# Graph attention on one core: first x tiles projected in two parts, row 0 spread by TensorE, adjacency turned later

## The chip, the cores and the metric

One core of one Trainium2 chip. The metric is the device time of one execution in microseconds (us), lower is better. The core's engines are TensorE (PE in the profile, its weight loads PEld), VectorE (DVE), ScalarE (ACT), GpSimd (POOL) and SyncE (SP), which issues DMAs.

## What is computed

```python
N, D_IN, H, DH, ALPHA, MASK_VAL = 2048, 512, 16, 32, 0.2, -65500.0
seq = (x @ W_seq).reshape(N, H, DH)
score1 = einsum('nhd,d->hn', seq, a1)
score2 = einsum('nhd,d->hn', seq, a2)
scores = leaky_relu(score1[:, :, None] + score2[:, None, :], negative_slope=ALPHA)
scores = scores + (1.0 - adj)[None, :, :] * MASK_VAL
attn = softmax(scores, axis=-1)
hidden = einsum('hij,jhd->ihd', attn, seq).reshape(N, D_IN)
out = layernorm(x + elu(hidden @ W_out + b_out), axis=-1)
```

x is 2048 x 512, adj is 2048 x 2048 of zeros and ones, all float32.

## The kernel before

All engines run programs written out by hand; they meet only through semaphores, and each engine executes its own program strictly in order. Nodes are cut into NT = 16 tiles of 128.

**First stage (to about 91 us), by tile t.** SP loads x tiles into a ring of six buffers and adjacency tiles (1 MB each) into a ring of four, after W (four chunks of 256 KB) and the two small broadcast loads of a1 and a2 (lines 219 and 220, between the first and the second chunk of W). VectorE and POOL multiply W by a1 and a2 (L514, L758) and VectorE sums the products over each head (L519) into 16 extra columns of each half of Wx, so that one product of x with Wx gives seq and both scores. For each tile:

- turn_x(t) on TensorE (L270) transposes x tile t, four 128x128 transposes into bank t % 2; ScalarE's copy_x (L406) brings it to xT.
- project(t) (L282) multiplies it by Wx: 8 matmuls of 272 columns in float32, recorded as 16 passes, each with a weight load. It waits for x_copied, for seq_copied of tile t - 2 (its PSUM banks), and at t = 0 for wa_ready of each k, that is for VectorE's sums.
- cast_adj(t) on ScalarE (L413) turns adjacency tile t to 8 bits and sums its rows; fix_adj(t) on VectorE (L525, L528) handles rows without edges.
- turn_adj(t) on TensorE (L292) transposes the tile, eight transposes, into bank 6 + t % 2; copy_adj(t) brings it to adj8, on VectorE for even tiles (L559), on ScalarE for odd ones (L419). turn_adj(t) waits for adj_fixed and, from t = 2 on, for the copy of tile t - 2 (adj_ready).
- copy_ab(t) and copy_seq(t) on VectorE (L534 to L543) empty the projection's banks; largest (L551, L553) follows each fourth tile.

TensorE's order is turn_x(t + 1), project(t), turn_adj(t). ScalarE's is copy_x(t + 1), cast_adj(t), and at even t copy_adj(t - 1). VectorE's is fix_adj(t), at odd t copy_adj(t - 1), copy_ab(t), copy_seq(t).

**Turn to the heads (91 to 103 us).** turn_a (L298) transposes the first score into rows, one per head; ScalarE copies them to aT (L431), SP stores aT to a DRAM scratch in four pieces (L230), waits for x_turned and the stores, and loads the row of head 0 back to all 128 partitions in four pieces of 256 KB (L234). Rows 1 to 15 follow as one load of 1 MB each (L241). aT lies in the first 16 partitions of row 1's buffer. Meanwhile the maxima go through TensorE (mx_turned, mx_spread; L318, L322), VectorE and ScalarE make E (L583, L437, L439) and Es (L595), VectorE writes the scale column of seq (L600), and values(0) (L605) makes the first value tile.

**Heads (to about 500 us).** For each head and tile, VectorE (L653) or ScalarE (L471) compares the head's row with a column of ab, VectorE ANDs the result with adj8 (L667), and TensorE multiplies by V (L332, mask_products), with adj_products (L344) between. split_high and split_low (L444, L611) make V. The last stage normalizes, multiplies by W_out (L394), and applies elu and the layer norm.

## Time and profile before

| | us |
|---|---|
| median of 3 runs | 570.86 |
| lowest, highest | 568.2, 571.78 |
| the profiled execution | 573.0 |
| its span | 571.1 |
| its mean granted clock of TensorE | 0.971 |

The span goes from the first to the last recorded instruction; the execution's own time has 1.9 us around it. Line numbers in the profile are those of the kernel before. An arrow in a row names what is written and what is read (tring<-abc,ab), "<-" behind idle time what ended it. Clock figures are tenths or shares of full speed, 1.0 being 2.4 GHz.

### The profile page before, as it was taken

How to read it: one execution, taken by the hardware profiler on the slowest of the kernel's cores; microseconds unless marked ns; L12 is line 12 of the kernel's file. 1: busy time of each engine (PE TensorE's matmuls, PEld its weight loads, DVE VectorE, ACT ScalarE, POOL GpSimd, SP SyncE). 2: the span in 40 equal slices, each digit the busy share in tenths (PEclk: the TensorE clock that was granted, in tenths of full speed). 3: DMA queues.
4: the chain of work that ended last, by engine and by line, in shares of the span. 5: the costliest groups of instructions: out<-in, count | busy, mean ns of one | idle time of the engine just before them, and what ended most of it. 6: DMA issues, size and time to landing. Idle time of an engine off the chain costs nothing.

```text
span 571.1 us, 15331 instructions
## 1 busy us (share of the span) xinstructions
PE 520.7 (91%) x6803; PEld 468.1 (82%) x6803; DVE 503.9 (88%) x804; ACT 420.7 (74%) x384; POOL 38.6 (7%) x63
## 2 busy tenths in 40 slices
PE   2999993757999999999999999999999999799992
PEld 2688882657999999999999999999999999544440
DVE  3878687999897969699999999989998979879997
ACT  1567684999696978799999998999996966122230
POOL 4000000000000000000000000000000000334432
PEclk9999997796999999999999999999999999899997
DMA  7988614010201202020211201102012030013433
GB/s 259 414 307 287 227 56 152 7 75 1 76 1 76 71 8 76 2 75 2 76 36 43 76 2 76 75 3 76 2 76 76 2 130 2 1 55 110 141 119 129
DMA packets 14194, 49.64 MB, mean 87 GB/s; under 512 B 1776, under 2 KB 2800, under 8 KB 10160
## 3 DMA queue, kind: packets, MB, share of 16 engines
q1 hardware_dynamic: 14128, 48.67, 23.9%
q8 instruction: 53, 0.87, 0.6%
q14 instruction: 13, 0.11, 0.1%
HBM read 44.34 MB, written 4.33 MB: 85 GB/s over the span
## 4 chain that ended last, share of the span: by engine, by line
PE 68%; DVE 19%; ACT 5%; issue 4%; DMA 2%; POOL 1%; SPq 1%; POOLq 0%; DVEq 0%; ACTq 0%
PE sums L332 38%; PE bank L344 19%; PE sums L282 6%; DVE tring L667 2%; ACT tring L471 2%; DVE tring L653 2%; PE sums L394 2%; DVE Vp L731 2%; DVE Vp L718 2%; DVE Vp L741 2%; DVE Vp L737 1%; DVE adj L559 1%; PE bank L292 1%; DMA abc<-a_rows 1%; ACT tring L413 1%
## 5 line engine op out<-in xcount | busy, mean ns | idle before, releaser
L471 ACT ACTIVATE tring<-abc,ab 128x2048 int8<-128x2048 f32 x157 | 304.2, 2003 | 4.6 <-DMA abc<-a_rows 4.6
L332 PE MATMUL sums<-Vp,tring 128*128 128x132 f16 x4096 | 257.5, 228 | 21.2 <-DVE Vp L611 10.0
L332 PEld LDWEIGHTS sums<-Vp,tring 128*128 128x128 fp8e4 x4096 | 252.4, 100 | 23.1 <-issue 18.3
L667 DVE TENSOR_TENSOR tring<-adj,tring 128x512 uint32<-128x512 uint32 x256 | 167.4, 690 | 10.5 <-ACT tring L471 10.3
L653 DVE TENSOR_SCALAR tring<-abc,ab 128x2048 int8<-128x2048 f32 x99 | 127.1, 1284 | 2.1 <-DMA abc<-a_rows 2.1
L344 PE MATMUL bank<-Vp,adj 128*128 128x132 f16 x2048 | 126.0, 221 | 0.9 <-ACT acc L450 0.9
L344 PEld LDWEIGHTS bank<-Vp,adj 128*128 128x128 fp8e4 x2048 | 122.3, 96 | 1.0 <-issue 1.0
L282 PE MATMUL sums<-Vp,abc 128*128 128x272 f32 x256 | 63.6, 401 | 1.2 <-DVE Vp L519 1.2
L394 PE MATMUL sums<-abc,Vp 128*128 128x512 f32 x128 | 59.2, 607 | 0.8
L282 PEld LDWEIGHTS sums<-Vp,abc 128*128 128x128 f32 x256 | 48.4, 195 | 11.4 <-DVE Vp L519 2.3
L506 ACT ACTIVATE Vp<-Vp 128x512 f32<-128x512 f32 x16 | 10.1, 631 | 50.1 <-DVE Vp L727 50.1
L461 ACT ACTIVATE low<-sums 128x66 f32<-128x66 f32 (+3 forms) x33 | 18.0, 596 | 38.5 <-PE sums L332 38.5
L394 PEld LDWEIGHTS sums<-abc,Vp 128*128 128x128 f32 x128 | 23.5, 194 | 26.8 <-issue 23.5
L626 DVE SCALAR_TENSOR_TENSOR cab<-low,sums 128x33 f32<-128x33 f32 (+3 forms) x66 | 23.3, 419 | 18.1 <-ACT low L461 18.1
L413 ACT ACTIVATE tring<-Vp 128x2048 int8<-128x2048 f32 x16 | 30.6, 1913 | 2.1 <-DMA Vp<-in_adj_dram 2.1
L406 ACT COPY abc<-sums 128x512 f32<-128x512 f32 x16 | 9.4, 586 | 30.4 <-PE sums L270 30.4
L763 POOL MEMSET Vp<- 128x128 f32 x1 | 0.2, 204 | 428.0 <-PE sums L332 428.0
L450 ACT ACTIVATE acc<-bank 128x132 f32<-128x132 f32 x64 | 16.9, 282 | 8.8 <-PE bank L344 8.8
L611 DVE SCALAR_TENSOR_TENSOR Vp<-Vp,xp 128x528 f16<-128x528 f16 (+1 forms) x34 | 21.3, 672 | 0.0
L605 DVE TENSOR_TENSOR xp<-acc,Es 128x1056 f32<-128x1056 f32 (+1 forms) x17 | 20.2, 1192 | 0.1
L270 PE MATMUL sums<-Vp,abc 128*128 128x128 f32 x64 | 10.7, 294 | 10.1 <-DMA abc<-in_x_dram 10.1
L444 ACT ACTIVATE Vp<-xp 128x528 f16<-128x528 f32 (+1 forms) x34 | 19.5, 634 | 0.0
(69 smaller groups left out, 304.0 us busy)
## 6 DMA issues: line engine op xcount, KB each, us to landing
Vp<-in_adj_dram SPq DMA_DIRECT2D x16, 1024.0 KB, 6.9
abc<-a_rows SPq DMA_DIRECT2D x15, 1024.0 KB, 4.6
abc<-in_x_dram SPq DMA_DIRECT2D x16, 256.0 KB, 6.3
Vp<-in_x_dram SPq DMA_DIRECT2D x16, 256.0 KB, 2.9
out_dram<-Vp SPq DMA_DIRECT2D x16, 256.0 KB, 2.2
Vp<-in_L_gnn_W_seq_dram SPq DMA_DIRECT2D x4, 256.0 KB, 6.2
abc<-a_rows SPq DMA_DIRECT2D x4, 256.0 KB, 3.7
abc<-in_L_gnn_W_out_dram SPq DMA_DIRECT2D x1, 1024.0 KB, 5.4
```

What stands on the lines that cost most here:

```text
L282: mm = pe.matmul(bank[2 + 2 * s + r][:, 0:WC], xT[:, r, k * P:(k + 1) * P], Wx[:, k, s, :], start=(k == 0), stop=(k == KT - 1))
L332: mm = pe.matmul(bank[b][:, 0:4 * BW].rearrange("p (v c w) -> p v c w", v=4, c=ITB)[:, :, c, :], slot(jt)[:, it * P:(it + 1) * P].bitcast( ...
L344: mm = pe.matmul(bank[6 + s % 2][:, 0:GRP * HW], adj8[:, jt, it * P:(it + 1) * P].bitcast(F8), Vp[:, GRP * g:GRP * (g + 1), jt, part, HW:V ...
L394: mm = pe.matmul(bank[q], hT[:, q, k * P:(k + 1) * P], Wo_sb[:, k, :], start=(k == 0), stop=(k == KT - 1))
L413: act.activation(tring[:, it, :], stage[:, it % STAGE, :], ACT.Copy, bias=BASE, scale=EDGE, accum_out=deg[:, r:r + 1]).then_inc(adj_cast, 1)
L444: high = act.activation(Vp[:, k, tiles, 0, s * HW:(s + 1) * HW], xp[:, tiles, s, :], ACT.Copy, scale=1.0 / LO[s])
L471: act.activation(slot(jt), row(h), ACT.Sign, bias=ab[:, jt, H + h:H + h + 1], scale=-1.0).then_inc(u_ready, 1)
L605: dve.tensor_tensor(xp[:, tiles], seq[:, tiles, k, :].unsqueeze(2).to_broadcast([P, n, 2, HW]), Es[:, tiles, :, k:k + 1].to_broadcast([P, ...
L611: low = dve.scalar_tensor_tensor(out=Vp[:, k, tiles, 1, s * HW:(s + 1) * HW], in0=Vp[:, k, tiles, 0, s * HW:(s + 1) * HW], scalar=-LO[s], ...
L626: both = dve.scalar_tensor_tensor(out=into, in0=lo, scalar=1.0 / LO[s], in1=high, op0=ALU.mult, op1=ALU.add)
L653: dve.tensor_scalar(slot(jt), row(h), ab[:, jt, H + h:H + h + 1], -1.0, ALU.is_gt, ALU.mult).then_inc(above, 1)
L667: dve.tensor_tensor(words, adj8[:, jt, :].bitcast(U32), words, ALU.bitwise_and).then_inc(t_ready, 1)
```

## The change

- **First tiles.** project() takes a range of columns. Tiles 0 and 1 are projected on their first 256 columns as soon as W and x are there, and the last 16 columns (a1, a2) follow for both, after turn_x(2). In the second part the matmuls don't wait for x again, and start=True is given once, in the first part. The loads of a1 and a2 are issued by ScalarE at its start instead of by SP.
- **Adjacency.** TURNS gives the adjacency tiles that TensorE turns at each t: none at 0 and 1, then tile t - 2 up to t = 5, two at t = 6 and at t = 7, and tile t from 8 on. The copies follow one iteration later in ScalarE's and VectorE's orders, behind cast_adj and fix_adj.
- **Row 0.** Each piece of aT's first row is multiplied by a row of ones on TensorE (spread_row0) and copied by ScalarE (copy_row0) into row(0). SP's four loads and its wait for x_turned go. Row 1's load waits for row0_spread. The maxima's transposes move from banks 0 and 1 to bank 6.
- **Scale column.** POOL writes the scale column of seq; VectorE waits for scales_set before values(0).

```diff
@@ -44,6 +44,8 @@
 
 FIVE, SIX, SEVEN = (1, 4, 7, 10, 13), (1, 4, 6, 9, 11, 14), (1, 3, 6, 8, 10, 12, 14)
 DVE_TILES = (SIX, SIX, SEVEN, SEVEN, SIX, SIX, SIX, FIVE, SIX, SIX, SIX, FIVE, SIX, SEVEN, SEVEN, SEVEN)
+
+TURNS = ((), (), (0,), (1,), (2,), (3,), (4, 5), (6, 7)) + tuple((t,) for t in range(8, NT))
 
 MID, MID_AT = 2, 7
 ROUNDS = (0, 5, 5, 6, 4, 4, 4, 4, 4, 4, 4, 4, 5, 5, 6, 0)
@@ -152,12 +154,12 @@
             sem(s) for s in ("x_turned", "x_copied", "seq_made", "ab_copied", "seq_copied"))
         adj_cast, noedge_set, adj_fixed, adj_turned = (sem(s) for s in ("adj_cast", "noedge_set", "adj_fixed", "adj_turned"))
         adj_ready = [sem("adj_ready0"), sem("adj_ready1")]
-        a_turned, a_copied = sem("a_turned"), sem("a_copied")
+        a_turned, a_copied, row0_spread, row0_copied = (sem(s) for s in ("a_turned", "a_copied", "row0_spread", "row0_copied"))
         a_stored = [sem(f"a_stored{c}") for c in range(4)]
         ones_set, mx_part, mx_ready, mx_turned, mcol_ready, diag_ready, mx_spread, Mb_ready = (
             sem(s) for s in ("ones_set", "mx_part", "mx_ready", "mx_turned", "mcol_ready", "diag_ready", "mx_spread", "Mb_ready"))
         e_in, e_out, r_sum, r_in, r_out = (sem(s) for s in ("e_in", "e_out", "r_sum", "r_in", "r_out"))
-        vsc_step, e_scaled = sem("vsc_step"), sem("e_scaled")
+        vsc_step, scales_set, e_scaled = sem("vsc_step"), sem("scales_set"), sem("e_scaled")
 
         xp_made, high_made, v_ready = sem("xp_made"), sem("high_made"), sem("v_ready")
 
@@ -197,7 +199,10 @@
 
         def row_loaded(eng, h):
 
-            eng.wait_ge(abc_loaded[h % 2], 16 * (h // 2 + 1) + (48 if h % 2 == 0 else 0))
+            if h == 0:
+                eng.wait_ge(row0_copied, 4)
+            else:
+                eng.wait_ge(abc_loaded[h % 2], 16 * ((h + 1) // 2))
 
 
         @block.sync
@@ -215,9 +220,6 @@
             load_x(0)
             for k in range(KT):
                 sp.dma_start(Wx[:, k, :, 0:half], W_seq[k * P:(k + 1) * P, :].rearrange("p (s c) -> p s c", s=2)).then_inc(w_loaded[k], 16)
-                if k == 0:
-                    sp.dma_start(a12[:, 0:DH], a1.rearrange("(o d) -> o d", o=1).partition_broadcast(P)).then_inc(a12_loaded, 16)
-                    sp.dma_start(a12[:, DH:2 * DH], a2.rearrange("(o d) -> o d", o=1).partition_broadcast(P)).then_inc(a12_loaded, 16)
             for t in range(1, XS - 2):
                 load_x(t)
             for t in range(NT):
@@ -228,11 +230,9 @@
             for c in range(4):
                 sp.wait_ge(a_copied, c + 1)
                 sp.dma_start(scratch[:, c * 512:(c + 1) * 512], aT[:, c * 512:(c + 1) * 512]).then_inc(a_stored[c], 16)
-            sp.wait_ge(x_turned, NT)
             for c in range(4):
                 sp.wait_ge(a_stored[c], 16)
-                sp.dma_start(row(0)[:, c * 512:(c + 1) * 512],
-                             scratch[0:1, c * 512:(c + 1) * 512].partition_broadcast(P)).then_inc(abc_loaded[0], 16)
+            sp.wait_ge(row0_spread, 4)
             for h in range(1, H):
                 if h == 1:
                     sp.wait_ge(seq_made, NT)
@@ -270,18 +270,23 @@
                     mm = pe.transpose(bank[r][:, k * P:(k + 1) * P], xs[:, t % XS, k * P:(k + 1) * P], idf)
                 mm.then_inc(x_turned, 1)
 
-            def project(t):
+            def project(t, columns=slice(0, WC)):
+
                 r = t % 2
-                pe.wait_ge(x_copied, t + 1)
-                if t >= 2:
-                    pe.wait_ge(seq_copied, t - 1)
+                if columns.start == 0:
+                    pe.wait_ge(x_copied, t + 1)
+                    if t >= 2:
+                        pe.wait_ge(seq_copied, t - 1)
                 for k in range(KT):
-                    if t == 0:
+                    if t == 0 and columns.start == 0:
+                        pe.wait_ge(w_loaded[k], 16)
+                    if t == 0 and columns.start > 0:
                         pe.wait_ge(wa_ready, 2 * k + 2)
                     for s in range(2):
-                        mm = pe.matmul(bank[2 + 2 * s + r][:, 0:WC], xT[:, r, k * P:(k + 1) * P], Wx[:, k, s, :],
-                                       start=(k == 0), stop=(k == KT - 1))
-                mm.then_inc(seq_made, 1)
+                        mm = pe.matmul(bank[2 + 2 * s + r][:, columns], xT[:, r, k * P:(k + 1) * P], Wx[:, k, s, columns],
+                                       start=(k == 0 and columns.start == 0), stop=(k == KT - 1), skip_group_check=(t < 2))
+                if columns.stop == WC:
+                    mm.then_inc(seq_made, 1)
 
             def turn_adj(it):
                 r = it % 2
@@ -300,10 +305,17 @@
                         mm.then_inc(a_turned, 1)
 
             turn_x(0)
-            for t in range(NT - 1):
+            project(0, slice(0, half))
+            turn_x(1)
+            project(1, slice(0, half))
+            turn_x(2)
+            for t in range(2):
+                project(t, slice(half, WC))
+            for t in range(2, NT - 1):
                 turn_x(t + 1)
                 project(t)
-                turn_adj(t)
+                for it in TURNS[t]:
+                    turn_adj(it)
             pe.wait_ge(x_copied, NT)
             pe.wait_ge(ab_copied, NT // 2)
             turn_a(range(0, NT // 2))
@@ -313,14 +325,22 @@
             turn_adj(NT - 1)
             pe.wait_ge(ab_copied, NT)
             turn_a(range(NT - 1, NT))
+            def spread_row0(c):
+
+                pe.wait_ge(a_copied, c + 1)
+                pe.matmul(turned_a[c], ones[0:1, :], aT[0:1, c * 512:(c + 1) * 512], start=True, stop=True).then_inc(row0_spread, 1)
+
+            pe.wait_ge(ones_set, 1)
+            spread_row0(0)
             pe.wait_ge(mx_ready, 1)
-            pe.wait_ge(a_copied, 1)
-            pe.transpose(bank[0][0:2 * H, 0:P], mx, idf).then_inc(mx_turned, 1)
-            pe.wait_ge(ones_set, 1)
+            pe.wait_ge(adj_ready[0], NT // 2)
+            pe.transpose(bank[6][0:2 * H, 0:P], mx, idf).then_inc(mx_turned, 1)
+            spread_row0(1)
             pe.wait_ge(diag_ready, 1)
-            pe.wait_ge(a_copied, 2)
-            pe.matmul(bank[1][:, 0:2 * H], ones[0:2 * H, :], diag[0:2 * H, :], start=True, stop=True).then_inc(mx_spread, 1)
-            pe.wait_ge(a_copied, 4)
+            pe.matmul(bank[6][:, 0:2 * H], ones[0:2 * H, :], diag[0:2 * H, :], start=True, stop=True).then_inc(mx_spread, 1)
+            spread_row0(2)
+            spread_row0(3)
+            pe.wait_ge(row0_copied, 4)
             pe.wait_ge(seq_copied, NT)
             pe.wait_ge(Mb_ready, 1)
             for s in range(2):
@@ -398,6 +418,9 @@
 
         @block.scalar
         def _(act):
+            act.dma_start(a12[:, 0:DH], a1.rearrange("(o d) -> o d", o=1).partition_broadcast(P)).then_inc(a12_loaded, 16)
+            act.dma_start(a12[:, DH:2 * DH], a2.rearrange("(o d) -> o d", o=1).partition_broadcast(P)).then_inc(a12_loaded, 16)
+
             def copy_x(t):
                 r = t % 2
                 act.wait_ge(x_turned, t + 1)
@@ -424,19 +447,29 @@
                 if t + 1 < NT:
                     copy_x(t + 1)
                 cast_adj(t)
-                if t % 2 == 0 and t > 0:
-                    copy_adj(t - 1)
+                if t > 0:
+                    for it in TURNS[t - 1]:
+                        if it % 2 == 1:
+                            copy_adj(it)
             def copy_a(c):
                 act.wait_ge(a_turned, c + 1)
                 act.copy(aT[:, c * 512:(c + 1) * 512], turned_a[c][0:H, :]).then_inc(a_copied, 1)
 
             for c in range(4):
                 copy_a(c)
+            def copy_row0(c):
+                act.wait_ge(row0_spread, c + 1)
+                act.copy(row(0)[:, c * 512:(c + 1) * 512], turned_a[c]).then_inc(row0_copied, 1)
+
             copy_adj(NT - 1)
+            copy_row0(0)
+            copy_row0(1)
             act.wait_ge(e_in, 1)
             act.activation(E[:, :, 1, :], E[:, :, 0, :], ACT.Exp, scale=-SLOPE).then_inc(e_out, 1)
             act.wait_ge(e_out, 1)
             act.activation(E[:, :, 0, :], E[:, :, 0, :], ACT.Exp, scale=-1.0).then_inc(e_out, 1)
+            copy_row0(2)
+            copy_row0(3)
 
             def split_high(k, tiles=slice(0, NT)):
                 act.wait_ge(xp_made, k + 2 if k > 0 else tiles.stop // (NT // 2))
@@ -561,8 +594,10 @@
 
             for t in range(NT):
                 fix_adj(t)
-                if t % 2 == 1:
-                    copy_adj(t - 1)
+                if t > 0:
+                    for it in TURNS[t - 1]:
+                        if it % 2 == 0:
+                            copy_adj(it)
                 copy_ab(t)
                 if t < NT - 1:
                     copy_seq(t)
@@ -573,11 +608,11 @@
             dve.tensor_reduce(mx, mxc.rearrange("p c k -> p k c"), AX.X, ALU.max).then_inc(mx_ready, 1)
             copy_seq(NT - 1)
             dve.wait_ge(mx_turned, 1)
-            dve.tensor_reduce(mcol[0:2 * H, :], bank[0][0:2 * H, 0:P], AX.X, ALU.max).then_inc(mcol_ready, 1)
+            dve.tensor_reduce(mcol[0:2 * H, :], bank[6][0:2 * H, 0:P], AX.X, ALU.max).then_inc(mcol_ready, 1)
             dve.wait_ge(mcol_ready, 1)
             dve.tensor_scalar(diag[0:2 * H, :], idf[0:2 * H, 0:2 * H], mcol[0:2 * H, :], None, ALU.mult).then_inc(diag_ready, 1)
             dve.wait_ge(mx_spread, 1)
-            dve.tensor_copy(Mb, bank[1][:, 0:2 * H]).then_inc(Mb_ready, 1)
+            dve.tensor_copy(Mb, bank[6][:, 0:2 * H]).then_inc(Mb_ready, 1)
             dve.wait_ge(Mb_ready, 1)
             Mrow = Mb[:, 0:H].unsqueeze(1).to_broadcast([P, NT, H])
             dve.tensor_tensor(E[:, :, 0, :], ab[:, :, H:2 * H], Mrow, ALU.add).then_inc(e_in, 1)
@@ -595,10 +630,9 @@
                 dve.scalar_tensor_tensor(out=Es[:, :, s, :], in0=E[:, :, s, :], scalar=LO[s],
                                          in1=vinv.unsqueeze(1).to_broadcast([P, NT, H]), op0=ALU.mult,
                                          op1=ALU.mult).then_inc(e_scaled, 1)
-
+            dve.wait_ge(e_scaled, 2)
+            dve.wait_ge(scales_set, 1)
             dve.wait_ge(seq_copied, NT)
-            dve.tensor_copy(seq[:, :, :, DH], vsc[:].unsqueeze(1).to_broadcast([P, NT, H])).then_inc(e_scaled, 1)
-            dve.wait_ge(e_scaled, 3)
 
             def values(k, tiles=slice(0, NT)):
                 n = tiles.stop - tiles.start
@@ -759,6 +793,10 @@
                                    Wx[:, k, :, 0:half].rearrange("p s (h d) -> p s h d", d=DH),
                                    a12[:, DH:2 * DH].unsqueeze(1).unsqueeze(1).to_broadcast([P, 2, H // 2, DH]), ALU.mult).then_inc(wa_prod[1], 1)
 
+
+            pool.wait_ge(vsc_step, 2)
+            pool.wait_ge(seq_copied, NT)
+            pool.tensor_copy(seq[:, :, :, DH], vsc[:].unsqueeze(1).to_broadcast([P, NT, H])).then_inc(scales_set, 1)
             pool.wait_ge(t_free, NT * (H - 2))
             pool.memset(idl, 0.0).then_inc(ident_l, 1)
             pool.wait_ge(ident_l, 1)
```

## Rows read from the trace of the kernel before

**Rows 1.** The page: busy times, clock in 40 slices, and one group (busy, mean ns)

```profile
PE 520.7 (91%) x6803; PEld 468.1 (82%) x6803; DVE 503.9 (88%) x804; ACT 420.7 (74%) x384; POOL 38.6 (7%) x63
...
PEclk9999997796999999999999999999999999899997
...
L282 PEld LDWEIGHTS sums<-Vp,abc 128*128 128x128 f32 x256 | 48.4, 195 | 11.4 <-DVE Vp L519 2.3
```

**Rows 2.** The chain of waits in order of time: start us, us, what

```profile
2.49 5.89 DMA adj<-in_L_gnn_a_dram
...
16.86 1.29 DVE Vp L519 x2
...
38.83 3.67 PE sums L282 x16
...
57.39 3.67 PE sums L282 x16
...
92.93 6.44 DMA abc<-a_rows
```

**Rows 3.** Timeline, 3 to 25 us: start, us, engine, line, tiles, shape, count, idle before

```profile
3.60 1.09 PE L270 MATMUL sums<-Vp,abc 128*128 128x128 f32 x4 [3.60 <-DMA abc<-in_x_dram]
...
11.18 1.11 PE L270 MATMUL sums<-Vp,abc 128*128 128x128 f32 x4 [6.49 <-DMA abc<-in_x_dram]
...
12.08 3.72 PE L282 MATMUL sums<-Vp,abc 128*128 128x272 f32 x8
...
16.28 1.19 PE L282 MATMUL sums<-Vp,abc 128*128 128x272 f32 x4 [0.48 <-DVE Vp L519]
...
19.61 0.43 PEld L270 LDWEIGHTS sums<-Vp,abc 128*128 128x128 f32 x4
19.66 0.61 PE L270 MATMUL sums<-Vp,abc 128*128 128x128 f32 x4
...
20.11 3.83 PE L282 MATMUL sums<-Vp,abc 128*128 128x272 f32 x16
...
24.69 3.83 PE L282 MATMUL sums<-Vp,abc 128*128 128x272 f32 x16
```

**Rows 4.** Timeline, one tile of the first stage, 75 to 83 us

```profile
75.99 0.59 ACT L406 COPY abc<-sums 128x512 f32<-128x512 f32 x1 [0.58 <-PE sums L270]
76.47 1.91 ACT L413 ACTIVATE tring<-Vp 128x2048 int8<-128x2048 f32 x1
...
79.33 2.29 DVE L559 TENSOR_SCALAR adj<-bank 128x2048 int8<-128x2048 int8 x1
...
79.47 0.62 PE L292 MATMUL bank<-Vp,tring 128*128 128x128 f16 x8
```

**Rows 5.** Timeline, 90 to 120 us

```profile
91.05 1.86 ACT L419 ACTIVATE adj<-bank 128x2048 int8<-128x2048 int8 x1
...
92.82 0.37 PE L322 MATMUL sums<-Vp 32*128 32x32 f32 x2 [0.87 <-issue]
...
94.36 0.42 ACT L439 ACTIVATE tring<-tring 128x256 f32<-128x256 f32 x1
...
95.99 1.33 DVE L605 TENSOR_TENSOR xp<-acc,Es 128x528 f32<-128x528 f32 x2
...
99.39 2.00 ACT L471 ACTIVATE tring<-abc,ab 128x2048 int8<-128x2048 f32 x1 [4.61 <-DMA abc<-a_rows]
...
103.15 5.17 PE L332 MATMUL sums<-Vp,tring 128*128 128x132 f16 x48 [9.96 <-DVE Vp L611]
...
119.25 4.92 PE L332 MATMUL sums<-Vp,tring 128*128 128x132 f16 x77 [2.75 <-DVE tring L667]
```

**Rows 6.** Busy time and granted clock by stretch

```profile
core 0: us, PE busy (x) PEld busy (x) DVE busy (x) ACT busy (x) POOL busy (x), PEclk, DMA share, GB/s
...
90.00:95.00 5.00, 1.19 (x12) 0.68 (x9) 3.96 (x17) 3.43 (x5) 0.00 (x0) 0.91 0.46 144
...
105.00:110.00 5.00, 4.85 (x60) 4.64 (x59) 5.00 (x6) 5.00 (x6) 0.00 (x0) 0.73 0.00 0
```

## The prediction, made before the changed kernel was seen

> **What bounds the kernel now.** I read the page first. TensorE is busy 91% of the span and VectorE 88% [rows 1], an average over stages with different limits, so I went to the chain of waits and read it in order of time. It has three parts that this change touches. First, up to 18 us it runs through the load of a1 and a2 (2.49 to 8.38) and then through VectorE, which sums W times a1 and W times a2 into the last 16 columns of each half of Wx; the last of those sums ends at 18.15 [rows 2]. TensorE has all of x tile 0 by 3.60 and does almost nothing with it, since project(0) waits for those columns [rows 3]. Second, from 20 to 90 us the chain is TensorE: one tile of project() every 4.64 us (38.83 to 57.39 is four tiles [rows 2]), against 3.67 for the 16 passes of project, 0.45 for turn_x and 0.46 for turn_adj, 4.58 in all. Third, after the last transposes of the a columns it goes out to DRAM and back: row 0 of the first head is complete in SBUF only at 92.93 + 6.44 = 99.37 [rows 2], ScalarE and VectorE start on it at 99.39, and TensorE's first mask product starts at 103.15 [rows 5]. Behind that ScalarE and VectorE bound head 0, and all later stages hang on it, so a shift of the start of head 0 shifts the end by as much.
>
> **The first tiles (lines 305 to 309, L282, L519).** Before, the passes of project(1) start at 20.11 and those of project(2) at 24.69 [rows 3]. Now only the last 16 columns wait for VectorE. TensorE turns x tile 0 at 3.60, ScalarE copies it by 5.3, W is landing, so project(0) on 256 columns starts at 5.3. Its pace decides the sum. The clock row of the page says 9 (full) from the start [rows 1], but the durations say otherwise: four transposes take 1.09 at 3.60 and 1.11 at 11.18 against 0.61 at 19.66, and eight passes take 3.72 at 12.08 where 16 take 3.83 at 20.11 [rows 3]. That is half pace, the lower of the two levels (1.2 against 2.4 GHz). At 16.28 four passes take 1.19, so full pace came at most 5.1 us after the steady work began at 11.18; after the restart at 103.15 the stretch 105 to 110 has a mean clock of 0.73, half until 107.7, which is 4.6 us [rows 5, 6]. I take 4.8 us at half pace, a loss of 2.4; bounds 3 and 6 us, losses 1.5 and 3.0.
>
> The Trainium skill, "TensorE: Matmul & The Clock Gate", Part 1, says that the throttled clock is the default and that activity releases it. By this rule the sum is the one I make; by the page's clock row taken at its word it would be 2.4 us better. The durations agree with the rule.
>
> A full-pace pass of 272 columns is 3.67/16 = 0.229, so one of 256 is 0.216 and a tile 3.45. Project(0) then ends at 5.3 + 3.45 + 2.4 = 11.15. Then turn_x(1) 0.45 (x tile 1 was there by 11.18 before [rows 3], and is not later now), a wait of 0.5 for ScalarE's copy of it, which has no matmul to hide behind, project(1) 3.45, turn_x(2) 0.45: 16.0.
>
> Now the narrow parts: 16 passes of 16 columns for each of two tiles, each with a full 128x128 weight load. The trace has no such pass. From below it costs its 16 columns alone, 0.013; from above the mean of one recorded weight load of L282, 0.195 [rows 1]. The nearest row is L270's: four such loads in 0.43 [rows 3], 0.11 each. I take 0.11, 1.75 a tile; the ends are 0.2 and 3.1 a tile. So 16.0 + 1.75 + 1.75 + turn_x(3) 0.45 puts project(2) at 19.95 instead of 24.69: 4.7 us earlier. Against project(0) and project(1) in one piece this splitting costs some 3 us more of TensorE.
>
> Is anything else late? VectorE's sums took 18.15 - 8.38 = 9.77 [rows 2]. With the two loads issued by ScalarE at about 0.7 and 1.3, and 5.9 us to land at worst, as before, they start at 7.2 and end at 17.0, when project(0)'s narrow part needs its last pair at 17.3. So the earlier load is enough in either case and its exact landing is worth nothing. copy_x(2) now waits for the narrow part of tile 0 (seq_made), 17.75, and is through by 18.3, before project(2). SP loses two issues ahead of W and x (1.0 us); that helps loads which TensorE doesn't wait for any more.
>
> **The adjacency turned later (TURNS).** The turns of adjacency tiles 0 and 1 leave the first tiles and come back as doubles at t = 6 and 7: 2 x 0.46 = 0.9 back. The 0.23 in four tiles that TensorE waited for fix_adj (18.56 - 4 x 4.58) goes in the tiles where the turn lags, two times: 0.45 gained. But the doubles meet a wait that the old order did not have. turn_adj(6) at t = 7 needs bank 6 empty, so copy_adj(4); tile 4 was turned at t = 6, and VectorE copies it in its iteration 7, behind fix_adj(7), which waits for cast_adj(7), which stands behind copy_x(8), which needs turn_x(8) of the same iteration. One such iteration of before shows the length: copy_x starts at 75.99, the cast at 76.47, VectorE's adj copy starts at 79.33, just when project ends (the turn at 79.47 follows it), and takes 2.29, some 2.2 to the next instruction [rows 4]. TensorE would therefore stand for 81.5 - 79.5 = 2.0 us at t = 7. The same holds at t = 8: turn_adj(8) needs copy_adj(6), which again stands behind fix_adj(8): another 2.0. turn_adj(5) at t = 6 needs ScalarE's copy_adj(3), behind cast_adj(6): 0.5 + 2.0 + 1.8 (1.86 for one in [rows 5]) = 4.3 after the turn, against project and the turn before it, 4.13: 0.2. From t = 9 on the order is the old one. Behind the waiting turn on TensorE stand turn_x(t + 1) and project(t + 1), so all 4.2 us are on the chain. Bounds: 0 (if ScalarE and VectorE run ahead) and 5.
>
> First stage: 4.7 - 0.9 + 0.45 - 4.2 = 0.05 us. The early start is given back.
>
> **Row 0 by TensorE.** Removed: SP's wait for x_turned and four loads of 256 KB, the last in at 99.37. Added: four spreads, each one matmul of 512 columns with a single row of ones. A 272-column matmul is two passes of 0.229, so one of 512 is 2 x 0.43 = 0.86, and twice that at half clock. Spread 0 runs from 90.6 to 91.4, 1 from 92.0 to 92.85, ahead of the matmul that was at 92.82 [rows 5], 2 to 94.1 and 3 to 95.0, or 95.8 if the clock has fallen. Then four ScalarE copies of 128x512 from PSUM, 0.5 each in a row (75.99 to 76.47 [rows 4]). copy_adj(15) ends at 92.9 [rows 5]; copies 0 and 1 run to 93.9; the two Exp as before, the second from 94.4 to 94.8; copies 2 and 3 to 95.9, or 96.4. So ScalarE starts on head 0 3.0 to 3.5 earlier than at 99.39. VectorE gives the seq column copy to POOL and waits for scales_set; behind that wait stands values(0), and POOL's one copy of 128x256 lies beside Exp and Es, which end at 95.6. So values(0) ends at 97.0 instead of 97.3, the first compare at 98.3; ScalarE's first mask is ready by 98.3 too, before at 99.39 + 2.00 = 101.4 [rows 5]. The first AND moves by 3.1 to 3.4. TensorE's new wait for row0_copied stands before the first mask product and is over by 96.4, when that product waits for V until 99.9. Row 1's load now waits for row0_spread, is issued at about 95 and is wanted after 120. Bounds of the gain: 2.1 (what VectorE waited there, 99.39 less 95.99 + 1.33 [rows 5]) and 3.5. I take 3.25.
>
> **Sum.** 0.05 + 3.25 = 3.3 us. The profiled execution took 573.0 (span 571.1 and 1.9 around it): 569.7 after. That execution lay 2.1 above the median of 570.86, so against the median 567.5 (0.6% faster).
>
> **Rivals.** (A) The turns don't wait: banks come free in time. For it: VectorE and ScalarE have idle time in their shares [rows 1]. Against: that idle comes from waiting for the cast and for TensorE, which is the very order that holds the copy back. Gain 3.3 + 4.2 = 7.5, time 563.3. (B) The narrow passes cost a whole recorded weight load, 0.2: 2 x 1.35 = 2.7 later, time 570.2. For it: the pipelined 0.11 comes from passes of 128 columns; against: nothing shows why width would make a load longer. (C) The clock is full from the start, or the narrow passes hide their loads: 2 us better, 565.5. (D) The slower one: in the two waits of 2.0 us at t = 7 and 8 the granted clock falls. It fell at 94.1 (mean 0.91 in 90 to 95 [rows 6]) after some 3.5 us with almost no work, and was half for 13.6 us until 107.7. Half clock over 13.6 us of the first stage, where TensorE is the bound, costs up to 6.8 us and makes 574.3; it decides the sign from 3.3 lost, that is 6.6 us at half. Against it: TensorE idled 2.75 before 119.25 [rows 5] with the clock at full there [rows 1].
>
> The Trainium skill, "TensorE: Matmul & The Clock Gate", section "HAM oscillation — how this bites in real kernels", says that waits between short bursts throttle the array and that each restart is paid for; by this rule D is what the new waits bring. The row at 119.25 doesn't show it for a wait of this length.
>
> **How the numbers follow.** Forecast 0.52 (567.5; its own range 565.5 to 569.5), A 0.15, C 0.13, B 0.12, D 0.08. Measurement tells about 1% (5.7 us) from no change. Faster by more needs below 565.15: A nearly whole, a part of C and a little of the forecast with the spread of runs (568.2 to 571.78): 0.22. Slower by more, above 576.6, only in the tail of D and from causes not seen: 0.06. The rest, 0.72, is within 1%. The range from A to the middle between B and D: 562.8 to 571.5.
>
> **What would show it.** Right: project(0)'s 256-column passes from about 5.3 at half pace, project(2) near 20; waits of about 2 us of TensorE before L292 (turn_adj) at t = 7 and t = 8, released by VectorE's adj copy; end of the first stage still near 90; the first L471 about 3.5 before its old 99.39, first mask product near 99.9. Wrong: no idle before L292; a narrow pass far from 0.11; the clock at 0.5 between 40 and 90 us; or values(0), not the row, late at the start of head 0.

## The result, and the profile after

The changed kernel takes 574.19 us (median of 7 runs, 573.61 to 575.81), the kernel before 571.78 in the same comparison (7 runs, 568.2 to 572.57): ratio 1.005, 95% interval 1.0029 to 1.0071. It is slower by some 2.4 us, where 3.3 us faster was forecast; the time lies outside the range. The profiled execution took 573.65 (span 571.9) against 573.0 (span 571.1) before, so the pair of profiles shows only 0.65 of the 2.4: the profiled execution of before lies 1.2 above its median, that of after 0.5 below.

The page after; the rows answer to [rows 1].

```profile
PE 529.0 (93%) x6843; PEld 475.3 (83%) x6843; DVE 504.0 (88%) x803; ACT 422.4 (74%) x388; POOL 39.3 (7%) x64
...
PEclk9899999787999999999999999999999999899997
...
L286 PEld LDWEIGHTS sums<-Vp,abc 128*128 128x128 f32 x288 | 53.8, 200 | 12.1 <-ACT abc L429 2.6
```

TensorE has 8 us more of busy time, of which the narrow passes are the visible part (L286 has 32 passes more than the old L282). The clock row has an 8 in the second slice, 14 to 29 us, where it had 9. The timeline of the first tiles, which answers to [rows 3]:

```profile
5.58 1.08 PE L270 MATMUL sums<-Vp,abc 128*128 128x128 f32 x4 [5.58 <-DMA abc<-in_x_dram]
...
7.94 5.95 PE L286 MATMUL sums<-Vp,abc 128*128 128x256 f32 x16 [1.28 <-DMA Vp<-in_L_gnn_W_seq_dram]
...
15.01 3.72 PE L286 MATMUL sums<-Vp,abc 128*128 128x256 f32 x16 [0.67 <-ACT abc L429]
...
19.00 3.64 PE L286 MATMUL sums<-Vp,abc 128*128 128x16 f32 x32
...
23.14 3.27 PE L286 MATMUL sums<-Vp,abc 128*128 128x272 f32 x7
```

The reader is to see four things. x tile 0 is turned at 5.58, not at 3.60. The first 256-column pass starts at 7.94, not 5.3, and the 16 passes take 5.95, near the forecast 3.45 + 2.4 for a start at half pace; the next 16, at full pace, take 3.72 and not 3.45. The 32 narrow passes take 3.6. And of the wide passes that follow, the seven from 23.14 take 3.27, 0.47 each, where one took 0.229 before. The chain of waits (start us, us, what), beside [rows 2], says what set these:

```profile
1.16 6.64 DMA Vp<-in_L_gnn_W_seq_dram
...
19.16 3.48 PE sums L286 x32
22.64 0.70 PE sums L270 x4
23.35 5.13 PE sums L286 x16
...
29.37 3.67 PE sums L286 x16
```

It begins with the first chunk of W: issued at 1.16, in at 7.80, where a1 and a2 had begun it before. Before, the same chunk took 3.3 us from its issue and was in at 4.5, so W is 3.3 us later and x tile 0 is 2.0 later, and W is what the first pass waits for. Then it is TensorE: the narrow passes 3.48 for 32, 0.109 each, then project(2) 5.13 against 3.67 for the next tile. Busy time and clock by stretch (us; PE, PEld, DVE, ACT, POOL busy; PEclk; DMA share; GB/s) give the reason for the 5.13:

```profile
0.00:5.00 5.00, 0.00 (x0) 0.00 (x0) 0.00 (x0) 1.28 (x1) 1.07 (x8) 1.00 0.22 57
...
20.00:30.00 10.00, 10.00 (x60) 8.66 (x60) 6.29 (x22) 5.51 (x8) 0.00 (x0) 0.83 1.03 417
45.00:60.00 15.00, 12.05 (x80) 9.61 (x78) 9.52 (x24) 10.72 (x11) 0.00 (x0) 1.00 0.63 208
```

The first of these stretches in the kernel before:

```profile
0.00:5.00 5.00, 1.09 (x4) 0.72 (x4) 0.00 (x0) 1.56 (x2) 1.07 (x8) 1.00 0.33 109
```

In 20 to 30 us the mean granted clock is 0.83, so 3.4 us were at the lower level, 1.2 GHz, just behind the 32 narrow passes. And in the first 5 us the DMA engines moved 57 GB/s with a share of 0.22, where the same stretch before had 109 GB/s and 0.33: they moved less and were far from busy.

The timeline around t = 6 to 8, which answers to [rows 4]:

```profile
47.48 0.61 PE L297 MATMUL bank<-Vp,tring 128*128 128x128 f16 x8 [0.32 <-ACT adj L442]
...
49.05 1.91 ACT L436 ACTIVATE tring<-Vp 128x2048 int8<-128x2048 f32 x1
...
51.91 2.29 DVE L592 TENSOR_SCALAR adj<-bank 128x2048 int8<-128x2048 int8 x1
...
54.34 1.05 PE L297 MATMUL bank<-Vp,tring 128*128 128x128 f16 x16 [2.13 <-DVE adj L592]
...
61.64 0.61 PE L297 MATMUL bank<-Vp,tring 128*128 128x128 f16 x8 [2.13 <-DVE adj L592]
```

The wait of 0.32 at t = 6 (released by ScalarE's copy, L442) and the two of 2.13 at t = 7 and 8 (released by VectorE's copy, L592) stand where the prediction put them. The first stage ends with the last transposed a column at 95.56, where it was 90.26 before: 5.3 us later. Then row 0 (beside [rows 5]):

```profile
95.56 0.27 PE L303 MATMUL sums<-Vp,ab 128*16 128x128 f32 x1
...
98.11 1.04 ACT L462 COPY abc<-sums 128x512 f32<-128x512 f32 x2
...
98.32 1.96 PE L331 MATMUL sums<-abc,Vp 1*128 1x512 f32 x4
...
99.98 1.05 ACT L462 COPY abc<-sums 128x512 f32<-128x512 f32 x2
...
101.03 1.33 DVE L639 TENSOR_TENSOR xp<-acc,Es 128x528 f32<-128x528 f32 x2
101.06 2.00 ACT L504 ACTIVATE tring<-abc,ab 128x2048 int8<-128x2048 f32 x1
...
105.12 4.64 PE L352 MATMUL sums<-Vp,tring 128*128 128x132 f16 x48 [4.84 <-DVE Vp L645]
```

From the last a column to ScalarE's first compare (L504) it is 5.50, before it was 99.39 - 90.26 = 9.13; to the first mask product 9.56, before 12.89. The row gains 3.3 us by the mask product (3.6 by the compare), and the first mask product comes 2.0 us later than before all the same: 5.3 - 3.3.

### The profile page after: what moved, and what is told of

It reads as the page before. It is cut to its first block, busy times and chain, and to the rows that moved or that the text cites. A ratio compares the mean times of both kernels' runs of the same rounds, so it can differ in the third digit from the quotient of the medians.

```text
span 571.9 us, 15415 instructions
## 1 busy us (share of the span) xinstructions
PE 529.0 (93%) x6843; PEld 475.3 (83%) x6843; DVE 504.0 (88%) x803; ACT 422.4 (74%) x388; POOL 39.3 (7%) x64
## 4 chain that ended last, share of the span: by engine, by line
PE 70%; DVE 17%; issue 6%; ACT 4%; DMA 1%; POOL 1%; POOLq 0%; SPq 0%; DVEq 0%; ACTq 0%
PE sums L352 40%; PE bank L364 19%; PE sums L286 7%; DVE tring L701 2%; ACT tring L436 2%; DVE tring L687 2%; PE sums L414 2%; DVE Vp L765 2%; DVE Vp L752 2%; DVE Vp L775 2%; DVE adj L592 2%; DVE Vp L771 1%; DMA Vp<-in_L_gnn_W_seq_dram 1%; PE sums L270 1%; PE bank L297 1%
## 5 line engine op out<-in xcount | busy, mean ns | idle before, releaser
L504 ACT ACTIVATE tring<-abc,ab 128x2048 int8<-128x2048 f32 x157 | 304.2, 2002 | 0.0
L286 PE MATMUL sums<-Vp,abc 128*128 128x272 f32 (+2 forms) x288 | 68.5, 392 | 2.0 <-DMA Vp<-in_L_gnn_W_seq_dram 1.3
L286 PEld LDWEIGHTS sums<-Vp,abc 128*128 128x128 f32 x288 | 53.8, 200 | 12.1 <-ACT abc L429 2.6
L592 DVE TENSOR_SCALAR adj<-bank 128x2048 int8<-128x2048 int8 x8 | 18.3, 2284 | 0.0
```

The lines of the kernel that those rows point to most:

```text
L286: mm = pe.matmul(bank[2 + 2 * s + r][:, columns], xT[:, r, k * P:(k + 1) * P], Wx[:, k, s, columns], start=(k == 0 and columns.start == 0) ...
L504: act.activation(slot(jt), row(h), ACT.Sign, bias=ab[:, jt, H + h:H + h + 1], scale=-1.0).then_inc(u_ready, 1)
L592: dve.tensor_scalar(adj8[:].rearrange("p (q s) n -> p q s n", s=2)[:, :, :, it * P:(it + 1) * P], turned, -BASE, None, ALU.add).then_inc(a ...
```

## The experiments

Each comparison has runs of the kernel before on the same chip; ratios are to that kernel. The changed kernel itself was timed only in the comparison above (574.19 against 571.78), so a difference to it goes across comparisons, whose medians of the kernel before lie between 571.46 and 572.18. The ratios are the safer measure, and the gain by them stands beside. "Last a column" is the end of the first stage.

**1. Row 0 alone.** The kernel before with row_loaded, spread_row0, copy_row0, bank 6 for the maxima and SP's part; nothing else.

```diff
-            sp.wait_ge(x_turned, NT)
             for c in range(4):
                 sp.wait_ge(a_stored[c], 16)
-                sp.dma_start(row(0)[:, c * 512:(c + 1) * 512], ...).then_inc(abc_loaded[0], 16)
+            sp.wait_ge(row0_spread, 4)
```

> The kernel before with the spread of row 0 alone (the first tiles, the turns and the scale column as before). Theory (the row gives 3.3 us and the first stage takes back more): 3.3 us faster than the kernel before, ratio 0.994, first L471-type compare 3.0 to 3.6 after... earlier than its old 99.39, first mask product near 99.9. Rival (the row was hidden, or head 0 ends no earlier): ratio 1.000.

Measured: 568.94 (10 runs), ratio 0.9949 (0.993 to 0.9968), 3.2 us below the 572.18 of the kernel before. Timeline of row_alone:

```profile
89.61 0.27 PE L299 MATMUL sums<-Vp,ab 128*16 128x128 f32 x1
...
95.12 2.00 ACT L488 ACTIVATE tring<-abc,ab 128x2048 int8<-128x2048 f32 x1
...
99.41 2.88 PE L341 MATMUL sums<-Vp,tring 128*128 128x132 f16 x24 [5.07 <-DVE Vp L628]
```

Last a column to first compare 5.51, to the first mask product 9.80, without the scale column on POOL (9.56 with it, in the changed kernel). The term of 3.25 stands; the rest of the change costs 5.6 us. How well a profile alone gives this term is another matter: in before_a12_act (run 6), whose row is loaded as in the kernel before, the same distance is 101.75 - 89.85 = 11.90 and not 12.89, so it moves by 1 us between profiles. The comparison of run 1, ten executions against 33, doesn't hang on this.

**2. The waits.** The changed kernel, VectorE's order turned round.

```diff
             for t in range(NT):
-                fix_adj(t)
                 if t > 0:
                     for it in TURNS[t - 1]:
                         if it % 2 == 0:
                             copy_adj(it)
+                fix_adj(t)
```

> The changed kernel with VectorE's copy of the turned adjacency ahead of fix_adj in each iteration. Theory (the two waits of 2 us at t = 7 and 8 cost their length): the waits of TensorE before its adjacency turns at t = 7 and 8 fall from about 2.1 to under 0.3, the first stage ends 3.9 us earlier than in the changed kernel, 574.2 becomes 570.3, ratio to the kernel before 0.997. Rival (something behind them is late anyway, such as the copies of tiles 7 and 8): under 1 us gained, ratio 1.004.

Measured: 570.66 (12 runs), ratio 0.9992 (0.9974 to 1.001), 3.5 us below the 574.19 of the changed kernel, 3.3 by the ratios. Timeline of copy_first:

```profile
48.50 2.28 DVE L592 TENSOR_SCALAR adj<-bank 128x2048 int8<-128x2048 int8 x1
...
53.22 0.61 PE L297 MATMUL bank<-Vp,tring 128*128 128x128 f16 x8 [0.32 <-ACT adj L442]
...
94.88 3.76 PE L331 MATMUL sums<-abc,Vp 1*128 1x512 f32 x4
```

VectorE copies at 48.50, before the cast of its iteration is done, and of the wait of 2.13 at t = 7 there is 0.32 left, for ScalarE's copy; at t = 8 there is none. The first stage ends at 92.22, 3.3 us earlier, with a start 0.25 later (8.19 instead of 7.94), so 3.6 of the 3.9 us of wait that went (2.13 + 2.13 - 0.32). The waits cost their length. Not all of it reached head 0 in this profile. TensorE was recorded busy for all of 90 to 95 us, from 91 on with transposes and spreads, and the clock fell at about 94.7 (0.97 in that stretch, 0.50 in the next five). The last two spreads took 3.76 where they took 1.96, and the first compare, at 99.29, came 7.07 behind the last a column instead of 5.50.

**3. Wide instead of narrow passes.** The changed kernel, first two tiles cut at column 144, so both parts are at least 128 columns.

```diff
+        CUT = half // 2 + H
-            project(0, slice(0, half))
+            project(0, slice(0, CUT))
 ...
-                project(t, slice(half, WC))
+                project(t, slice(CUT, WC))
```

> The changed kernel with the first two tiles cut at column 144 instead of 256, so the later part has 128 columns. Theory (the 32 narrow passes cost their weight loads, 0.109 each, and let the granted clock fall at 20 to 30 us): wide passes cost no more than the narrow ones, the first part gets 3.4 us shorter and is then held by VectorE's sums until 17.6, project(2) starts 1.5 to 2 us earlier; if the clock also stays at full, 1.7 us more: 2.2 to 3.9 us faster than the changed kernel, ratio 0.998 to 1.001. Rival (the clock falls at its own time whatever the passes are): at most 2.2 us faster, and the clock mean of 20 to 30 us stays near 0.83.

Measured: 571.09 (12 runs), ratio 0.9992 (0.9973 to 1.0011), 3.1 us below the changed kernel, 3.3 by the ratios. By stretch, cut144:

```profile
20.00:30.00 10.00, 10.00 (x64) 8.73 (x63) 6.93 (x24) 7.35 (x9) 0.00 (x0) 1.00 1.02 411
...
45.00:60.00 15.00, 11.42 (x64) 9.39 (x64) 8.57 (x17) 8.51 (x8) 0.00 (x0) 0.89 0.57 202
```

The clock stays at full in 20 to 30 us. But in 45 to 60 us it is 0.89: it fell for 3.4 us, from about 51.7, in the wait at t = 7, which ends at 51.82. That is rival D, at a quarter of its price. The profiled execution took 573.75, the highest of the twelve (from 569.67), and ends the first stage at 94.24 against 95.56, so the pair of profiles shows 1.3 us there and nothing at the end; the gain is that of the medians.

**4. a1 and a2 by one partition.** ScalarE loads 128 B each into partition 0, TensorE spreads them with the row of ones, ScalarE copies them to a12; VectorE sets ones first.

```diff
-            act.dma_start(a12[:, 0:DH], a1.rearrange(...).partition_broadcast(P)).then_inc(a12_loaded, 16)
+            act.dma_start(a12[0:1, 0:DH], a1.rearrange("(o d) -> o d", o=1)).then_inc(a12_loaded, 16)
 ...
+            pe.matmul(bank[7][:, 0:2 * DH], ones[0:1, :], a12[0:1, :], start=True, stop=True).then_inc(a12_spread, 1)
```

> The changed kernel with a1 and a2 loaded to one partition (two loads of 128 B) and spread to all by one TensorE matmul and a ScalarE copy. Theory (the 256 small packets of the two broadcast loads beside x tile 0 and W hold those back): x tile 0 is turned at 3.6 instead of 5.58, the first 256-column pass starts at about 5.3 instead of 7.94, the first stage ends 2.3 us earlier, 574.2 becomes 571.9, ratio 1.000. Rival (W or x is late for another reason, as two queues at once): the first pass stays near 7.9 and the time at 574.2.

Measured: 572.3 (12 runs), ratio 1.0019 (0.9999 to 1.0038), 1.9 us below the changed kernel, 1.8 by the ratios. The two intervals overlap (the changed kernel's begins at 1.0029), so this gain alone is not clear of noise. TensorE's timeline of a12_by_pe:

```profile
4.16 1.11 PE L271 MATMUL sums<-Vp,abc 128*128 128x128 f32 x4
...
5.95 5.14 PE L287 MATMUL sums<-Vp,abc 128*128 128x256 f32 x16 [0.67 <-ACT abc L435]
...
12.20 3.72 PE L287 MATMUL sums<-Vp,abc 128*128 128x256 f32 x16 [0.68 <-ACT abc L435]
...
16.20 4.20 PE L287 MATMUL sums<-Vp,abc 128*128 128x16 f32 x32
...
53.19 1.86 PE L298 MATMUL bank<-Vp,tring 128*128 128x128 f16 x16 [2.13 <-DVE adj L597]
```

x tile 0 is turned at 4.16, behind the spread of a1 and a2, and the first 256-column pass starts at 5.95 instead of 7.94 (expected 3.6 and 5.3). There are still two DMAs on ScalarE's queue, but of 128 B each instead of 256 rows of 128 B, and the DMA engines move 179 GB/s in the first 5 us instead of 57. In this profile the clock took it back:

```profile
10.00:20.00 10.00, 9.32 (x61) 8.45 (x60) 6.76 (x14) 4.44 (x5) 0.61 (x1) 0.95 1.02 421
20.00:30.00 10.00, 10.00 (x43) 8.20 (x44) 4.80 (x16) 4.86 (x7) 0.00 (x0) 0.70 1.02 413
...
45.00:60.00 15.00, 12.55 (x75) 10.16 (x73) 8.33 (x21) 9.50 (x9) 0.00 (x0) 0.89 0.58 186
```

It was at half for 6.8 us from about 19.1, inside the narrow passes (16.20 to 20.40), and for 3.4 us from the end of the wait at t = 7, and the first mask product came at 105.15, as in the changed kernel (105.12). This execution (575.19) is the slowest of the twelve: eight took 571.8 to 572.5 with a mean clock of 0.966 to 0.974, four 574.7 to 575.2 with 0.963. So the clock doesn't do the same in every execution; where it differed in the eight, no profile shows.

**5. Each adjacency tile in its own turn.** The changed kernel with TURNS = (t,) for all t, tiles 0 and 1 turned behind the narrow part.

> The changed kernel with each adjacency tile turned in its own turn again (tiles 0 and 1 behind the later part of the first two projections), so no double turns. Theory (the delayed turns as written cost more than they bring): no wait over 0.5 us of TensorE before an adjacency turn, first stage 2.5 us shorter than in the changed kernel, 571.7, ratio to the kernel before 0.9995. Rival (delaying the turns is what lets tiles 0 to 2 go on, and without it VectorE or the adjacency loads hold them): 574 or more.

Measured: 570.77 (12 runs, 568.96 to 573.8), ratio 1.0001 (0.9978 to 1.0024) to the 571.46 of this comparison. TensorE's timeline of turns_each:

```profile
18.18 1.86 PE L286 MATMUL sums<-Vp,abc 128*128 128x16 f32 x16
...
20.33 2.83 PE L286 MATMUL sums<-Vp,abc 128*128 128x16 f32 x16
23.60 1.04 PE L297 MATMUL bank<-Vp,tring 128*128 128x128 f16 x8 [0.44 <-DVE tring L562]
```

The one wait before an adjacency turn is 0.44. The first stage ends at 92.12, 3.4 us earlier than in the changed kernel, although the clock is at half for 6.8 us from about 21.1: the second 16 narrow passes take 2.83 where the first took 1.86. The delayed turns as written cost some 3 us (2.8 by the ratios, 3.4 by the medians).

**6. The two loads moved, nothing else.** The kernel before with a1 and a2 loaded by ScalarE.

> The kernel before with only the two broadcast loads of a1 and a2 moved to the start of ScalarE's queue. Theory (256 packets of 128 B beside x tile 0 and W delay both): x tile 0 is turned at 4.8 to 5.6 instead of 3.6 and the first chunk of W is there only at about 7.9, so VectorE's sums start at 7.9 instead of 8.4; since nothing waited for x tile 0 in this kernel, it gains that 0.5 us: ratio 0.999. Rival (the late start in the changed kernel comes from the removed SP issues or from TensorE's new order): x tile 0 at 3.6 and sums from about 5, ratio 0.994.

Measured: 570.3 (12 runs), ratio 0.9987 (0.9967 to 1.0007). Timeline of before_a12_act:

```profile
5.79 1.08 PE L267 MATMUL sums<-Vp,abc 128*128 128x128 f32 x4 [5.79 <-DMA abc<-in_x_dram]
...
8.01 0.69 DVE L514 TENSOR_TENSOR acc<-Vp,adj 128x512 f32<-128x512 f32 x1 [8.01 <-DMA Vp<-in_L_gnn_W_seq_dram]
```

x tile 0 at 5.79 and W at 8.01, without any other edit, and 60 GB/s in the first 5 us. The move alone delays x by 2.2 us and W by some 3.5, and here that is hidden: the sums start 0.4 earlier than before. The time is within noise of the kernel before.

**7 and 8. The repairs together.** all_fixed has the edits of experiments 2, 3 and 4; fixed_turns_each those of 3, 4 and 5.

> The changed kernel with three repairs: a1 and a2 through one partition and TensorE, the cut at column 144, VectorE's copies ahead of fix_adj. Theory (the four terms add: late start 2.3, narrow passes 3.4 and the clock's fall 1.7, waits 3.9, against a row gain of 3.3): first stage 4 us shorter than in the kernel before, 564.8, ratio 0.987. Rival (TensorE's clock takes part of it back in another place of the stage, as it did in a12_by_pe at 19 to 26 and 53 to 57 us): 567 to 568, ratio 0.992.

> As all_fixed, but with each adjacency tile turned in its own turn and VectorE's order as it is. Theory: the delay of the turns, once its waits are gone, is worth 1.8 us, so 566.6, ratio 0.990. Rival (the delay brings nothing, since the turns are work of TensorE wherever they stand): within 0.5 us of all_fixed.

Measured: all_fixed 563.78 (6 runs), ratio 0.988 (0.9852 to 0.9907); fixed_turns_each 565.94 (6 runs), ratio 0.9915 (0.9895 to 0.9935). all_fixed, TensorE's timeline and the stretches:

```profile
5.57 3.88 PE L288 MATMUL sums<-Vp,abc 128*128 128x144 f32 x16 [0.68 <-ACT abc L436]
...
10.56 2.23 PE L288 MATMUL sums<-Vp,abc 128*128 128x144 f32 x16 [0.68 <-ACT abc L436]
...
15.04 2.50 PE L288 MATMUL sums<-Vp,abc 128*128 128x128 f32 x20 [0.47 <-DVE Vp L560]
```

```profile
20.00:30.00 10.00, 10.00 (x62) 8.40 (x61) 8.22 (x24) 6.86 (x9) 0.00 (x0) 1.00 1.02 414
...
45.00:60.00 15.00, 14.58 (x94) 11.79 (x92) 12.06 (x29) 11.10 (x12) 0.00 (x0) 1.00 0.67 230
```

The first tiles start at 5.57, the later parts are held by VectorE's sums until 15.04, and the clock is at full throughout. all_fixed beats both kernels. It is 2.2 us below fixed_turns_each in the same comparison (the intervals just overlap), where 1.8 was expected for the delay of the turns. The profiles give the delay only part of that: the first stage ends at 85.12 against 86.06, 0.9 us; another 0.5 comes before the first mask product (94.47 against 95.87), where the last two spreads took 2.63 in fixed_turns_each and 1.96 in all_fixed.

**9 and 10. Which of the two makes the clock fall.** a12_by_pe with one repair each: that of experiment 2 (pe_copy_first) and that of 3 (pe_cut144).

> a12_by_pe with VectorE's copies ahead of fix_adj, narrow passes kept. In a12_by_pe the granted clock fell twice in the first stage, at 19 to 26 us and again at 53.2, in the wait at t = 7. Theory (the second fall comes from that wait, the first from the narrow passes): no fall between 30 and 90 us, the fall at about 19 to 26 stays; against a12_by_pe 3.9 us for the waits and 1.7 for the clock, 572.3 becomes 566.7 to 568.4. Rival (the clock falls there anyway): a fall of 3.4 us between 45 and 60 us stays, and the time is 568.4 or more.

> a12_by_pe with the cut at column 144, waits kept. Theory (narrow passes are what lets the clock fall before 30 us): full clock from about 9 us until the wait at t = 7, where it may fall for 3.4 us in some executions; against a12_by_pe some 3.4 us for the passes held only by VectorE's sums and up to 3.4 for the clock, so 566.5 to 569. Rival (the clock falls at 20 us by itself): it is at half for 3 to 7 us between 15 and 30 us, 570 or more.

Measured: pe_copy_first 569.22 (10 runs), ratio 0.9961 (0.9938 to 0.9985); pe_cut144 569.41 (10 runs), ratio 0.9966 (0.9943 to 0.9989). The times are 0.8 and 0.4 above the expected ranges, and that of pe_copy_first lies where its rival had it (568.4 or more); the clock decides between the two. By stretch, pe_copy_first and then pe_cut144:

```profile
20.00:30.00 10.00, 10.00 (x50) 8.30 (x51) 7.55 (x19) 5.55 (x8) 0.00 (x0) 0.87 1.02 415
...
45.00:60.00 15.00, 14.58 (x97) 11.93 (x95) 13.61 (x29) 10.99 (x11) 0.00 (x0) 1.00 0.68 239
```

```profile
20.00:30.00 10.00, 10.00 (x61) 8.42 (x60) 7.92 (x22) 7.14 (x9) 0.00 (x0) 1.00 1.02 415
...
45.00:60.00 15.00, 11.39 (x66) 9.25 (x65) 9.29 (x21) 7.83 (x8) 0.00 (x0) 0.89 0.47 160
```

In the first stage they split cleanly. Without the waits and with narrow passes the clock falls only in the stretch of these; with wide passes and the waits only in the stretch of the waits. Over all profiles with the changed order: each of the five with narrow passes has a fall in 15 to 30 us (changed kernel, copy_first, turns_each, a12_by_pe, pe_copy_first), none of the four without (cut144, pe_cut144, all_fixed, fixed_turns_each). In the first two it comes at 22.8 and 23.0, within 0.2 us behind the last narrow pass, in the other three at 21.1, 19.1 and 19.2, while the narrow passes run; it moves with them, and the four without them, whose first tiles start alike, hold full clock to 45 us and beyond. The wait at t = 7 brings a fall in three of four profiles (cut144, a12_by_pe, pe_cut144, not the changed kernel), in the wait or within 0.3 us of its end; the wait at t = 8, of 1.5 to 2.1 us, brings none in any of the four, and none of the profiles without these waits has a fall in 30 to 85 us.

A third place is the spread of row 0. In six of the ten profiles that have it the last two spreads take 1.96; in turns_each and fixed_turns_each they take 2.49 and 2.63, in copy_first and pe_cut144 3.76, since the clock fell before or while they ran. pe_cut144 ends the first stage 5.8 us earlier than a12_by_pe (89.81 against 95.61) and starts the first compare only 3.9 earlier (97.22 against 101.11). That is 1.9 us, enough for the 0.4 by which its time lies above the expected range; pe_copy_first has no such loss, and its 0.8 stays open.

## Why the prediction was wrong

By its own steps:

- **"TensorE turns x tile 0 at 3.60 ... project(0) on 256 columns starts at 5.3": this step failed.** It was 5.58 and 7.94, 2.64 us late, with W in at 7.80 where the step has it "landing". I reckoned only when a1 and a2 would land ("its exact landing is worth nothing") and what SP's queue loses; I did not count what their packets do beside x tile 0 and W when they run at the same time. Every instruction that a moved step issues counts, and its transfers too. Run 6 shows the delay with the move alone, run 4 shows most of it gone with the packets (4.16 and 5.95). All five profiles with the two broadcast loads on ScalarE's queue have x tile 0 at 4.78 to 5.79 and W at about 7.8 to 8.2.
- **The half pace at the start was right** (2.4 forecast; 5.95 is 2.5 more than the forecast tile and 2.2 more than the measured one of 3.72), and so was reading it from the durations against the page's clock row.
- **The wide passes were sized a little low.** The step took the price of a pass as proportional to its columns, 0.216 for 256. A tile of them took 3.72 at full pace (3.72 in a12_by_pe too), 0.27 more; project(0) took 0.1 more than forecast, and the wait for ScalarE's copy of x tile 1 0.67 instead of 0.5.
- **The narrow passes were right in duration** (0.11; 3.48/32 = 0.109) **and incomplete in effect: this is the second step that failed.** The step went from their end straight to a project(2) at full pace. They let the clock fall: project(2) took 5.13 and turn_x(3) 0.70 instead of 3.67 and 0.45, 1.7 us, which no term and no rival held; rival D had a fall only in the waits.
- **The delayed turns were right**: 0.2, 2.0 and 2.0 forecast, 0.32, 2.13 and 2.13 measured. Run 2 gives back 3.5 us (3.3 by the ratios), against 3.9 expected.
- **The row was right**: 3.25 forecast, 3.3 in the profile, 3.2 in run 1. That it came so near owes something to luck, since the distance it shortens moves by 1 us between profiles, and by up to 1.9 with the clock during the spreads (runs 2 and 10).
- **VectorE's sums were no bound**, as said: they started at 7.91, ended at 17.6, and TensorE's second part, from 19.0, was not held by them.

In the profile the miss at the first mask product is 2.0 + 3.25 = 5.2 us: 2.64 for the late start, 1.7 for the clock, 0.5 for the wider passes and the copy in the first tiles, 0.4 for the waits being longer, which is the whole within 0.1. From there to the end the changed profile is 1.2 us shorter than the one before (466.8 against 468.0). Of this 0.3 is gained by the start of head 1 (134.34 against 132.66), and 0.6 in its first 128 products, which took 9.95 instead of 10.56, with a mean clock of 0.66 against 0.58 in 130 to 140 us. The other 0.3 is not assigned, and neither is the 1.8 us by which the medians are further apart than the profiles.

The range has a slip of its own: the middle between B (570.2) and D (574.3) is 572.3, not 571.5. The measured time lies outside either.

Of the rivals, A (no waits) and C (full clock) didn't happen. B had the wrong price. D did not happen in the changed kernel's own profile. In three others with the same wait it did, but small: 3.4 us at half instead of 13.6, which costs 1.7. "TensorE: Matmul & The Clock Gate" of the Trainium skill, section "HAM oscillation — how this bites in real kernels", was the warning: waits between bursts throttle the array. The runs bear it out for the wait at t = 7, in three of four profiles, and not for the wait at t = 8. They also show that 32 passes of 16 columns, with TensorE 100% busy in the record, bring a fall too, while they run or within 0.2 us of their end. My counter-evidence, the idle of 2.75 before 119.25 at full clock, was one execution's. The changed kernel's profile has the same idle, and there the clock fell at about 121.8 (0.94 in 120 to 122 us, 0.50 in the next two):

```profile
120.92 7.55 PE L352 MATMUL sums<-Vp,tring 128*128 128x132 f16 x96 [2.75 <-DVE tring L701]
```

The Trainium skill, "DMA: Bandwidth & Descriptors", section "Issuing engines are not separate DMA queues", says that DMAs of different engines share the same 16 DMA engines and interleave, so that issuing from a second engine saves issue time alone. The trace agrees on the saving: SP had issued the last chunk of W by 3.84 instead of 4.82. It also shows a price that those sentences don't give: x tile 0 came 2.0 us and the first chunk of W 3.3 us later. I had weighed the queue only as an order of issues.

What stays open: why 256 rows of 128 B cost x and W so much when the DMA engines had a share of only 0.22. Run 4 takes away their number and most of their bytes at once, and no run issues them on ScalarE's queue after x and W. Open too is why the wait at t = 7 brings a fall and the one at t = 8 none, and whether POOL's scale column gave anything by itself; it was not run alone, and the 9.56 against 9.80 of run 1 bounds it at some 0.2 us, less than the profiles differ.

## What to carry to other kernels

When a small load moves to another engine's queue, ask which large loads it now runs beside; 32 KB in 256 packets held back the first pass by 2.6 us, and a load of one partition spread by one matmul with a row of ones gave 2.0 of it back. When a matmul is cut so that part of it can start early, keep both parts wide: 144 and 128 columns did the work of 256 and 16 and gained some 3 us. When a producer is allowed to lag and catches up by two, look for the buffer that its copy frees: the copy must stand ahead of, not behind, the work that waits for the next input.

## What was not expected of the hardware

- A busy TensorE can lose its clock. In the changed kernel it was recorded busy for all of 20 to 30 us and was granted 0.83; the five profiles with 16-column passes show such a fall, 3.4 or 6.8 us long, and those with 128-column passes don't. In copy_first it also fell at about 94.7, behind transposes and matmuls with one row of ones, all recorded busy.
- Waits of about the same length do not do the same: 2.13 us at t = 7 brought a fall in three of four profiles, 1.5 to 2.1 us at t = 8 in none of them.
- The clock at the start is not what its row says. The row has 1.0 from 0 us, while 16 passes took 5.95 from 7.94 and 3.72 from 15.01.
- Moving two loads of 16 KB each from SP's queue to ScalarE's lowered the DMA rate of the first 5 us from 109 to 57 GB/s.
